# Reordering the first two phases of a fused Mamba-style SSM and butterfly FFN kernel, and transposing the x-projection by the transpose path

## What is computed

```python
xz = einsum('bld,ed->ble', layernorm(x), in_proj_w); x_inner, z = split(xz, 2)
x_conv = silu(depthwise_causal_conv(x_inner, conv_w) + conv_b)     # 4 taps, 512 channels
x_dbl = einsum('bld,ed->ble', x_conv, x_proj_w)                    # 33 columns: delta, B, C
h = h * exp(delta*A) + x_t * (delta*B);  y_t = h . C               # scan over 2048 steps
x = x + ((y + x_conv*D) * silu(z)) @ out_proj_w.T
h = layernorm(x) @ W_exp + b_exp                                   # 256 -> 1024
h = gelu(butterfly(h, up_weights) + up_bias)                       # 10 stages of 2x2 mixes
x = x + butterfly(h, down_weights) @ W_con + b_con + down_bias     # 1024 -> 256
```

## Time and profile before

| | |
|---|---|
| median of 3 runs | 567.76 us |
| profiled execution: device time / span | 569.59 us / 567.9 us |
| TensorE busy | 528.9 us (93%) |
| VectorE busy | 409.6 us (72%) |
| ScalarE busy | 306.1 us (54%) |
| GpSimd busy | 109.5 us (19%) |
| mean granted TensorE clock | 0.966 |

### The profile page before, as it was taken

How to read it: one execution, slowest core, us unless ns; L and a number is a source line. 1 busy time by engine, 2 the same in 40 slices (tenths; PEclk the granted TensorE clock), 3 DMA queues, 4 the chain that set the end, 5 groups by cost and what they waited for, 6 DMA issues and landing times.

```text
span 567.9 us, 8152 instructions
## 1 busy us (share of the span) xinstructions
PE 528.9 (93%) x2996; PEld 430.3 (76%) x2996; DVE 409.6 (72%) x860; ACT 306.1 (54%) x526; POOL 109.5 (19%) x96
## 2 busy tenths in 40 slices
PE   3998899888999999999999999999999999699896
PEld 3766676776897779887888778877888788578886
DVE  4859999587983799468966799379946894575532
ACT  2876883865239622874268623962287417431342
POOL 4042100230201301050103120130105021411110
PEclk9986979799999999999999999999999999799999
DMA  8542311200012001210112001200021002100011
GB/s 244 97 27 3 80 35 38 76 2 2 23 52 74 4 2 48 66 39 2 37 41 74 0 9 68 71 8 1 5 73 38 0 2 74 41 1 0 6 34 37
DMA packets 42619, 21.75 MB, mean 38 GB/s; under 512 B 26419, under 2 KB 41011, under 8 KB 42580
## 3 DMA queue, kind: packets, MB, share of 16 engines
q1 hardware_dynamic: 39940, 17.57, 13.0%
q10 hardware_dynamic: 2640, 3.67, 2.3%
HBM read 16.78 MB, written 4.46 MB: 37 GB/s over the span
## 4 chain that ended last, share of the span: by engine, by line
PE 48%; DVE 20%; issue 12%; ACT 9%; SPq 6%; POOL 3%; DMA 0%; DVEq 0%; ACTq 0%; POOLq 0%
PE wide L711 12%; PE acc L844 9%; PE wide L833 7%; SPq L420 5%; PE wide L822 4%; DVE xc L1552 2%; DVE xc L1555 2%; POOL x1b_xn L598 2%; DVE state L1516 2%; DVE hid_low L1429 2%; PE wide L804 2%; PE small L731 2%; PE wide L811 2%; DVE xc L1412 2%; ACT L1054 2%
## 5 line engine op out<-in xcount | busy, mean ns | idle before, releaser
L1054 ACT ACTIVATE hid_f<-wide,bias_up 128x512 f32<-128x512 f32 x64 | 44.0, 687 | 162.0 <-PE wide L833 161.6
L1412 DVE SCALAR_TENSOR_TENSOR xc<-xi,taps,xc 128x512 f32<-128x512 f32 x96 | 87.0, 911 | 4.0 <-ACT xc L1085 1.7
L844 PE MATMUL acc<-w_down_high,hid_high 128*128 128x256 f32 x256 | 73.2, 286 | 5.6 <-DVE hid_low L1429 5.4
L844 PE MATMUL acc<-w_down_high,hid_low 128*128 128x256 f32 x256 | 71.9, 281 | 0.0
L844 PE MATMUL acc<-w_down_low,hid_high 128*128 128x256 f32 x256 | 71.9, 281 | 0.0
L1429 DVE TENSOR_TENSOR hid_low<-hid_f,hid_high 128x512 fp32r<-128x512 f32 x64 | 46.3, 725 | 29.8 <-ACT hid_high L1163 29.2
L833 PE MATMUL wide<-xnT_ln2T_high,w_up_high 128*128 128x512 f32 x128 | 55.4, 432 | 3.4 <-DVE xnT_ln2T_low L1423 1.8
L522 POOL TENSOR_TENSOR rstd<-var_eps,minus_half 128x4 f32<-128x4 f32 x16 | 19.1, 1192 | 202.8 <-DVE var_eps L1317 202.8
L711 PE MATMUL wide<-xnT_ln1T_high,w_in_high 128*128 128x512 f32 x128 | 56.5, 441 | 1.1 <-DVE xnT_ln1T_low L1423 1.0
L822 PE MATMUL wide<-w_out,xc 128*128 128x256 f32 x256 | 56.7, 379 | 0.3 <-DVE xc L1555 0.3
L844 PEld LDWEIGHTS acc<-w_down_high,hid_high 128*128 128x128 f32 x256 | 48.0, 188 | 11.2 <-issue 8.2
(11 more groups left out here) (185 smaller groups left out, 1054.6 us busy)
## 6 DMA issues: line engine op xcount, KB each, us to landing
x_res<-in_L_attn_x_dram SPq DMA_DIRECT2D x9, 512.0 KB, 3.5
c_near<-c_of_tokens SPq DMA_DIRECT2D x8, 512.0 KB
out_dram<-x1b_xn SPq DMA_DIRECT2D x8, 512.0 KB, 2.9
x_ln<-in_L_attn_x_dram SPq DMA_DIRECT2D x7, 512.0 KB, 3.6
xc<-in_L_attn_in_proj_w_dram ACTq DMA_DIRECT2D x2, 512.0 KB, 7.1
xc<-in_L_ffn_W_exp_dram ACTq DMA_DIRECT2D x1, 1024.0 KB, 10.8
x1b_xn<-in_L_ffn_W_con_dram ACTq DMA_DIRECT2D x1, 1024.0 KB, 14.5
raw_out<-n_L_attn_out_proj_w_dram ACTq DMA_DIRECT2D x1, 512.0 KB, 7.0
```

Source lines behind the costliest of these rows:

```text
L844: last = pe.matmul(acc[:, c, :], hid[h][:, j % HRING, c * P:(c + 1) * P], w_down[w][:, j, 0:DM], start=j == 0 and c % 2 == 0 and n == 0, s ...
L1054: ins = act.activation(out_ap, in_ap, how.pop("func"), **how)
L1412: ins = dve.scalar_tensor_tensor(xc[u % BATCH][:, e, :], xi[:, e, tap:tap + TILE], taps[:, e, tap:tap + 1], xc[u % BATCH][:, e, :], ALU.mu ...
```

## The change

The `fold` matrix goes: the x projection is brought token first by four full transposes, and `take_xd` adds the two halves with a reduction that takes the place of its copy. VectorE's wait for the cleared tiles moves from `constants()` to behind `take_xd(0)`. In phase 0, unit 1 is transposed before the FFN weight products, `step_sums(0)` comes ahead of step 6, and the DOWN mixing is placed between the convolutions of unit 1 on VectorE. The first two UP mixing stages move from phase 0 to phase 1, where they stand with the third; steps 15 and 16 follow later in phase 1.

```diff
@@ xd_tokens_first (TensorE), take_xd and constants (VectorE)
-                    last = pe.matmul(bank[:, c * P:c * P + XD], xdT[:, c * P:(c + 1) * P], fold[:, :], start=True, stop=True)
+                    last = pe.transpose(bank[:, c * P:(c + 1) * P], xdT[:, c * P:(c + 1) * P], ident[:, :])
-                mark_read(dve.tensor_copy(xd[:, :, :], tile_of("xdtok", 0, u)[:, :]
-                                          .rearrange("p (c w) -> p c w", w=P)[:, :, 0:XD]), "xdtok", 0, u)
+                mark_read(dve.tensor_reduce(xd[:, :, :], tile_of("xdtok", 0, u)[:, :]
+                                            .rearrange("p (c h w) -> p c w h", h=2, w=HALF)[:, :, 0:XD, :], AXIS_X, ALU.add), "xdtok", 0, u)
-                dve.tensor_tensor(fold[:, :], ident[:, 0:XD], ident[:, HALF:HALF + XD], ALU.add).then_inc(folded, 1)
@@ first_phase (TensorE)
-                pe.wait_ge(folded, 1)
                 xd_tokens_first(0)
+                transposes(1, "ln1T", x_ln, norm1)
                 prepare(4)
                 prepare(5)
-                prepare(6)
-                transposes(1, "ln1T", x_ln, norm1)
                 pe.wait_ge(masks_made, 2)
                 pe.wait_ge(zeroed, 2)
                 step_sums(0)
+                prepare(6)
                 in_projection(1, 0)
-                prepare(7)
                 in_projection(1, 1)
                 decayed_b(0)
+                prepare(7)
+                in_projection(1, 2)
+                in_projection(1, 3)
                 prepare(8)
-                in_projection(1, 2)
                 decayed_c_start(0)
                 prepare(9)
-                in_projection(1, 3)
+                in_projection(1, 4)
                 decayed_c_block(0)
                 prepare(10)
-                in_projection(1, 4)
+                in_projection(1, 5)
                 state_inputs(0)
                 prepare(11)
-                in_projection(1, 5)
-                prepare(12)
                 in_projection(1, 6)
                 off_diagonal(0)
+                prepare(12)
                 in_projection(1, 7)
                 prepare(13)
                 ssm_output(0)
-                prepare(14)
-                transposes(2, "ln1T", x_ln, norm1)
                 wait_all_taken("w_out")
                 out_projection(0, 0)
+                transposes(2, "ln1T", x_ln, norm1)
+                prepare(14)
                 out_projection(0, 1)
@@ phase 1 (TensorE): step 15 from behind in_projection 5 to behind state_inputs,
@@ step 16 from behind in_projection 6 to behind off_diagonal, the wait for w_down behind up 2
-                if place == "in 5":
+                if place == "state inputs":
                     prepare(15)
-                elif place == "in 6":
+                elif place == "products":
                     prepare(16)
-                elif place == "products":
                     wait_all_taken("w_up")
                 elif place == "up 1":
                     prepare(17)
+                elif place == "up 2":
                     wait_all_taken("w_down")
@@ first_phase (ScalarE)
                 exp_abs(0)
+                high_parts(1, "ln1T")
                 prepare(4)
                 prepare(5)
+                place_halo(1)
+                exp_sums(0)
                 scale_blocks(DOWN, 0)
-                place_halo(1)
-                high_parts(1, "ln1T")
-                exp_sums(0)
-                scale_blocks(DOWN, 1)
                 first_tap(1, 0)
-                scale_blocks(DOWN, 2)
                 first_tap(1, 1)
                 exp_gaps(0)
...
+                scale_blocks(DOWN, 1)
+                prepare(9)
+                copy_z(1, 4)
                 take_c_block(0)
...
+                scale_blocks(DOWN, 2)
                 silu_x(1)
                 silu_z(1)
-                scale_blocks(UP, 0)
-                scale_blocks(UP, 1)
                 high_parts(2, "ln1T")
@@ phase 1 (ScalarE): UP 0 behind exp_abs, UP 1 behind exp_sums, UP 2 behind copy_z 5 (before: UP 2 behind exp_abs)
                 if place == "abs":
+                    scale_blocks(UP, 0)
+                elif place == "sums":
+                    scale_blocks(UP, 1)
+                elif place == "gaps":
                     scale_blocks(UP, 2)
@@ first_phase (VectorE)
                 take_xd(0)
+                dve.wait_ge(zeroed, 2)
                 softplus(0)
-                multiply_short_paths(UP)
-                sum_biases()
                 low_parts(1, "ln1T")
                 take_sums(0)
+                sum_biases()
+                weigh(0)
+                multiply_short_paths(UP)
+                weigh_b(0)
                 add_blocks(DOWN, 0)
-                add_blocks(DOWN, 1)
                 multiply_whole_paths(UP)
-                weigh(0)
-                add_blocks(DOWN, 2)
-                weigh_b(0)
-                for e in range(CB):
-                    convolve(1, e)
+                convolve(1, 0)
                 diagonal_times_c(0)
                 sum_diagonal(0)
+                convolve(1, 1)
+                add_blocks(DOWN, 1)
+                convolve(1, 2)
+                advance_state(0)
                 assemble(0)
-                advance_state(0)
-                multiply_short_paths(DOWN)
+                convolve(1, 3)
                 first_stats(2)
                 gate(0, 0)
                 gate(0, 1)
-                first_normalise(2)
                 gate(0, 2)
                 gate(0, 3)
+                first_normalise(2)
+                multiply_short_paths(DOWN)
+                add_blocks(DOWN, 2)
                 multiply_whole_paths(DOWN)
-                add_blocks(UP, 0)
-                add_blocks(UP, 1)
+                low_parts(2, "ln1T")
                 first_residual(0, 0)
                 first_residual(0, 1)
                 second_stats(0)
-                low_parts(2, "ln1T")
                 second_normalise(0)
@@ phase 1 (VectorE): UP 0 behind softplus and ahead of low_parts(ln2T); UP 1 and UP 2 behind weigh_b
                 if place == "softplus":
+                    add_blocks(UP, 0)
+                elif place == "weighed":
+                    add_blocks(UP, 1)
                     add_blocks(UP, 2)
-                elif place == "weighed":
                     low_of_ffn(("w_up", 0, 0), ("w_up", 0, 1), ("w_up", 1, 0), ("w_up", 1, 1))
```

More of the change, by code:

```diff
@@ L148, in bass_preln_ssm_butterfly_ffn @@
         w_x = sb("w_x", [P, CB, HALF])
-        fold = sb("fold", [P, XD])
         w_out = sb("w_out", [P, CB, DM])
@@ L320, in bass_preln_ssm_butterfly_ffn @@
         rates_exp = sem("rates_exp")
-        folded = sem("folded")
         made = sem("made")
@@ L922, in phase @@
                 in_or_none(v, 5)
-                beside("in 5")
                 decayed_c_start(u)
                 in_or_none(v, 6)
-                beside("in 6")
                 decayed_c_block(u)
                 state_inputs(u)
+                beside("state inputs")
                 in_or_none(v, 7)
@@ L935, in phase @@
                 up(p, 2)
+                beside("up 2")
                 down(p, 0)
@@ L1171, in first_phase @@
                 exp_abs(0)
+                high_parts(1, "ln1T")
                 prepare(4)
                 prepare(5)
+                place_halo(1)
+                exp_sums(0)
                 scale_blocks(DOWN, 0)
-                place_halo(1)
-                high_parts(1, "ln1T")
-                exp_sums(0)
-                scale_blocks(DOWN, 1)
                 first_tap(1, 0)
-                scale_blocks(DOWN, 2)
                 first_tap(1, 1)
                 exp_gaps(0)
-                prepare(8)
+                exp_diagonal(0)
                 first_tap(1, 2)
-                take_c_start(0)
-                exp_diagonal(0)
-                prepare(9)
                 first_tap(1, 3)
                 save_halo(1)
+                prepare(8)
+                take_c_start(0)
+                scale_blocks(DOWN, 1)
+                prepare(9)
+                copy_z(1, 4)
                 take_c_block(0)
                 prepare(10)
-                copy_z(1, 4)
+                copy_z(1, 5)
                 copy_first_state(0)
+                silu_z(0)
                 prepare(11)
-                copy_z(1, 5)
+                copy_z(1, 6)
                 prepare(12)
-                copy_z(1, 6)
                 copy_z(1, 7)
-                silu_z(0)
+                scale_blocks(DOWN, 2)
                 silu_x(1)
                 silu_z(1)
-                scale_blocks(UP, 0)
-                scale_blocks(UP, 1)
                 high_parts(2, "ln1T")
@@ L1224, in phase @@
                 exp_sums(u)
+                beside("sums")
                 if v < UNITS:
@@ L1229, in phase @@
                     copy_z(v, 5)
+                beside("gaps")
                 take_c_start(u)
                 exp_diagonal(u)
```

(13 more changed lines are left out.)

## The result

The changed kernel takes 578.79 us (median of 4 runs, 577.98 to 581.41) beside 567.57 us for the kernel before (4 runs, 566.22 to 569.14): a ratio of 1.0205 (of the means), interval 1.0161 to 1.0248. So it is slower beyond doubt, and about 2% is its size. I had predicted 574.0 us. The sign was right, the size was not: +11.2 us where I had +6.2, and 578.79 lies 0.3 us above the upper end of my range.

What follows compares the result with a forecast made beforehand. Bound: VectorE's chain in phase 0, TensorE in settled phases. 2.5 (D) + 4.9 (UP) + 1.5 (clock) - 2.4 (transposes) = +6.5, taken as +6.2: 574.0 us on the median of 567.76; 80% range 565.5 to 578.5.

Steps and rivals of the forecast that it cites:

- The two waits: VectorE waits for `c_near` until 65.9 us in phase 0; TensorE's step 15 waits 5 us or more in phase 1.
- the half clock behind the gap: Phase 1, TensorE behind its wait for the UP mixing: half clock until it recovers, costing 1.5 us (0 to 3.8).
- the rest of phase 1 behind `down`: End of phase 1, after `down`: the forecast's sum had no term for it.
- D: Start of `take_xd(1)`, where VectorE in phase 0 hands over to phase 1; predicted 2.5 us later (0.5 to 3.0).
- The wait for `c_near`: Phase 0, VectorE ahead of the diagonal: waits from about 59.5 to 65.9 us, so `ssm_output(0)` starts at 80.8, 4.3 late.
- UP in phase 1: UP 1 and 2 mixed behind `weigh_b(1)` hold up step 15; `up` starts 4.9 us later against D (4.0 to 5.5).
- Transposes: Four transposes replace the fold's eight records on TensorE: 0.48 us less in each of phases 2 to 6, 2.4 together.
- a shared recovery of the clock: The two clock terms, in phases 0 and 1, may share one recovery, so the sum +6.5 was taken as +6.2.
- The faster one: Phase 0 is a chain of VectorE work and loses 6.4 us of it: 563.9 us, or 559.0; chance 0.20.
- The same: Clock stays up in both gaps and UP costs 4.0: +1.1, 568.9 us, within 0.3%; chance 0.09.
- Transposes and the clock: Transposes in a row bring TensorE to half clock, losing 1.7 us in each of 6 phases: 584 us; chance 0.03.
- the early unit 1: Start of phase 0: anything won or lost by the new order is gone at the wait for `c_near`; no gain counted.

Runs made afterwards that it cites:

- c_early: The changed kernel with the two transfers of `spread_c(0)` issued ahead of the 14 transfers of low DOWN weights; 572.44 us, ratio 1.0091.
- c_early_down0: `c_early` with DOWN 0 and the whole UP paths ahead of `weigh_b(0)` on VectorE; 571.3 us, ratio 1.0051.
- low_first: `early_unit1` with `low_parts(2)` ahead of the first residual, as in the changed kernel; 564.26 us, ratio 0.9932.
- filler: The changed kernel with 22 unused matmuls on TensorE ahead of step 15 in phase 1; 576.77 us, ratio 1.0172.
- up_moved_alone: The kernel before with only UP 0 and UP 1 moved into phase 1; 577.25 us, ratio 1.015.
- up_back: The changed kernel with UP 0 and UP 1 mixed in phase 0 again; 577.35 us, ratio 1.0178.
- fold_alone: The kernel before with only the fold replaced by four transposes and the reduction; 566.4 us, ratio 0.9974.
- early_unit1: The kernel before with the fold's transposes and unit 1's transposes, high and low parts, sums and weighing early; mixing order as before; 562.92 us, ratio 0.9916.
- early_up_moved: `early_unit1` with UP 0 and UP 1 moved into phase 1 as in the changed kernel; 571.27 us, ratio 1.0051.

## Why the prediction fell short, step by step

The two waits and the order in which they end were right; what failed is the sizing of the sum. The term for the half clock behind the gap, 1.5 us, measured 2.5 in this trace, and the rest of phase 1 behind `down`, put at nothing, measured 0.95. The mixing and D were 0.6 and 0.8 too small.

- *The wait for `c_near`, and D.* Right in place: L1529 waits 6.74 us for the transfer, and `ssm_output(0)` starts at 82.17 (I had 80.8), with 4.49 us idle ahead of it. The arrival was misread: the data stopped moving at 66 in both traces, but VectorE was let go at 67.22 only. The clock was misread too. I expected the gap to halve it and 2 us of that to show; the half clock lies there in before and in `c_early` without a gap, it is absent in `c_early_down0` and `low_first`, and the first pair took 5.0 us, 1.5 over the 3.5 of full clock. So +1.3 and -0.5 make the term +3.3 where I had +2.5; that it came so near is in part luck.
- *UP in phase 1.* Right: step 15 is D + 22.2 (I had 22.1), behind two blocks of mixing, and nothing else sets `up`. The last leg was 0.5 us too short: the filler has 6.2 us from step 15 to `up` at full clock, I had added up 5.7. So the term is 5.5 where I had 4.9, its upper bound.
- *The clock.* The step that was furthest off: 1.5 us of "0 to 3.8", where the filler measures 2.5, and the row of step 15 shows the doubling. I had let the clock recover within a stretch of 4.1 us; in this trace the half clock reached 5.7 us into it. The trace of before had a row for that, beyond those of the earlier trace rows: behind its gap of 2.09 us the clock stays at a half until 109.5.

```profile
106.00:108.00 2.00, 2.00 (x7) 1.52 (x6) 1.66 (x12) 2.00 (x6) 0.00 (x0) 0.50 0.17 16
108.00:110.00 2.00, 2.00 (x8) 1.58 (x7) 0.80 (x6) 1.97 (x6) 1.32 (x2) 0.62 0.28 72
```

  In four other executions the same gap cost 1.2 to 1.7 us, so 1.5 was not a bad value for the kernel, and the 2.5 belongs in part to this execution.
- *Behind `down`.* I called the order the same, and said nothing of what comes behind it. It is 0.95 us longer, and it comes with the moved UP: 34.34 us in `up_moved_alone`, 33.37 in `up_back`, 33.37 in `fold_alone`. 0.75 of it lies between `down` and the next `up` matmuls, 0.41 of that a wait of the second `ssm_output` blocks for VectorE's gate (L1551). The wait of 0.71 us for `hid_low` at 149.84 ends where `down` begins and is not part of it. Why the gate is late was not taken apart.
- *Transposes.* -2.1 us in phases 2 to 6 for my -2.4, and -1.4 in the timed kernel `fold_alone`.
- *The sum.* 3.3 + 8.0 - 0.2 + 0.95 - 2.1 = +9.9 on the traces, for +6.2: each term was off by 0.3 to 1.0 and all to the same side, but for the 0.2 ahead of `down`. I then took 0.3 off the sum for a shared recovery of the clock, which did not exist, since the two half clocks lie 44 us apart.
- *The range.* Its upper end was the sum of the terms' upper bounds on the profiled time, put on a median. The profiled executions of before and after lie 2.0 and 0.7 us above their medians, and the median of after itself is only known to about 0.5%. There was no room for either.
- *The rivals.* The faster one was refuted where it stood: UP's 6.44 us in phase 0 cost next to nothing (`up_moved_alone`, D -0.45). "The same" needed the clock to stay up; it didn't, and with a clock that does (`filler`) the kernel is still 1.7% slower. Transposes and the clock: refuted by `fold_alone`, and the run of 44 by the traces.
- *What I did not see.* I wrote that the time of UP "is not won" in phase 0, and left the late DOWN order at that. With UP in place it costs 14.4 us, of which the late `c_near` makes 6.7; the rest, by my reading, is DOWN 2 and UP behind the gates, where there is cover for one. With UP moved, as in the change, it costs 7.5, nearly all of it `c_near`. And the early unit 1, which I counted at nothing, is worth 3.5 us (3.3 by the ratios).

## What to carry to other kernels

A busy engine is not a path: before you credit or charge work that moves, find what would start earlier if it were gone, and test that with the one move alone. When an order lets a consumer come earlier, read when the queue asked for its data; here 17.7 us of small DMA issues ahead of one transfer of 512 KB turned an earlier start into a 6.7 us wait. Before you blame a half clock on a gap, look whether the kernel without the gap has it too. And when several moves lean on the same cover, price them together, in a two by two table.

## What the runs showed of the chip

- Runs of one kernel can follow their granted clock. The 12 runs of `c_early_down0` go from a span of 565.9 us at a mean clock of 0.981 to 573.1 us at 0.970, some 6 us for 0.01, with a correlation of -0.92. Its profile lies 3.7 us below the median of its runs. It is not so for every order of work: the 5 runs of `early_unit1` go from 560.1 us at 0.984 to 562.4 at 0.972, and the 7 of `early_up_moved` show no relation.
- Unneeded matmuls in a gap of 5.4 us kept the clock at 1.00, and the stretch behind it was 2.5 us shorter. But a half clock doesn't need a gap: in before it goes from 75.4 to 82.2 us, with TensorE busy in each microsecond since 70, behind the start of step 13, whose matmuls have few rows.
- The 14 issues of small pieces (4 KB) of the low DOWN weights hold SyncE's queue for 17.66 us, 1.26 us each, before the next transfer can be asked for.
- The last bytes of `c_near` moved before 66.0 us, and VectorE, whose wait it ended, was let go at 67.22: data that has stopped moving is not yet data that can be read.
